# Rows of maxima in the second attention: one transfer inside SBUF in place of two through DRAM, and their transposition two pairs of score products later

## The reference, cut to what matters

```python
qw = split_heads(q @ Wq + bq); kw = split_heads(k @ Wk + bk); vw = split_heads(v @ Wv + bv)
scores = jnp.einsum('bhqd,bhkd->bhqk', qw, kw) * inv_sqrt_d
weights = jax.nn.softmax(scores, axis=-1)
ctx = jnp.einsum('bhqk,bhkd->bhqd', weights, vw)
ctx = ctx.transpose(0, 2, 1, 3).reshape(B, S, D_MODEL)
return ctx @ Wo + bo
```

## Time and profile before

| | |
|---|---|
| median of 3 runs | 1082.23 us (1081.29 to 1084.33) |
| the profiled execution, its own time | 1093.17 us |
| its span | 1091.1 us |
| mean granted clock of TensorE in it | 0.911 of full |
| TensorE, VectorE, ScalarE busy | 87%, 66%, 42% of the span |

### The profile page before, as it was taken

One profiled execution on the slowest core, in us unless ns is written; L12 is line 12 of the kernel. 1 busy time (PEld: TensorE's weight loads), 2 busy tenths in 40 slices (PEclk: granted clock), 3 DMA queues, 4 the chain that ended last, 5 costly groups with the idle time before them and its releaser, 6 DMA issues.

```text
span 1091.1 us, 19956 instructions
## 1 busy us (share of the span) xinstructions
PE 951.9 (87%) x6592; PEld 586.3 (54%) x6592; DVE 725.4 (66%) x1959; ACT 459.0 (42%) x1022; POOL 222.4 (20%) x198
## 2 busy tenths in 40 slices
PE   5989998998987999999998678889899787877785
PEld 3656666574754887888854433234343242345564
DVE  5473868578798666666644676687848776464676
ACT  4354543234225443444423203576646456622222
POOL 0313320101112443443210010100100011113453
PEclk9989999898988999999999956999959797788998
DMA  8541020026183111111126861722611036243231
GB/s 298 182 164 69 1 78 0 20 59 174 59 288 108 50 46 55 46 51 50 44 96 159 150 141 23 120 37 62 108 28 40 21 84 170 78 155 89 81 102 33
DMA packets 70239, 98.63 MB, mean 90 GB/s; under 512 B 8796, under 2 KB 57183, under 8 KB 67712
## 3 DMA queue, kind: packets, MB, share of 16 engines
q1 hardware_dynamic: 60000, 61.67, 20.7%
q0 software_dynamic: 10144, 35.69, 12.0%
HBM read 71.04 MB, written 27.15 MB: 90 GB/s over the span
## 4 chain that ended last, share of the span: by engine, by line
PE 61%; DVE 22%; ACT 6%; DMA 4%; issue 3%; another core or an unknown queue 2%; SPq 0%; ACTq 0%; POOLq 0%; DVEq 0%
PE pb L1050 11%; PE pb L1070 7%; PE pb L1162 4%; PE pb L883 4%; PE pb L1071 4%; PE pb L1186 3%; PE pb L1140 3%; PE pb L836 3%; PE pb L872 3%; PE pb L892 3%; PE pb L813 3%; PE pb L849 3%; DVE MX L2051 2%; PE pb L807 2%; ACT EX L1477 2%
## 5 line engine op out<-in xcount | busy, mean ns | idle before, releaser
L2051 DVE TENSOR_REDUCE MX<-pb 128x1 f32<-128x512 f32 x256 | 160.5, 683 | 47.0 <-PE pb L1140 45.7
L1415 ACT ACTIVATE m<-pb,b1m 128x128 f32<-128x128 f32 x404 | 114.9, 369 | 173.4 <-PE pb L1050 143.6
L1477 ACT ACTIVATE EX<-pb 128x512 f32<-128x512 f32 x256 | 137.0, 600 | 105.4 <-PE pb L1186 104.1
L1050 PE MATMUL pb<-xt,w1h 128*128 128x128 f16 x1616 | 157.3, 221 | 5.9 <-issue 3.8
L1070 PE MATMUL pb<-w,mh 128*128 x404 | 150.0, 381 | 10.1 <-DVE ml L1948 9.5
L1050 PEld LDWEIGHTS pb<-xt,w1h 128*128 x1616 | 120.4, 99 | 43.7 <-issue 8.3
L1050 PE MATMUL pb<-xt,w1l 128*128 128x128 f16 x808 | 113.2, 221 | 1.4 <-issue 1.3
L1071 PE MATMUL pb<-w,ml 128*128 x404 | 110.4, 273 | 0.4 <-issue 0.4
L807 PE MATMUL pb<-identh 128*128 128x512 f16 x373 | 96.7, 413 | 15.3 <-DVE identh L1585 7.4
L1186 PE MATMUL pb<-QS,KS 49*128 49x512 f32 x256 | 80.3, 505 | 13.3 <-ACT EX L1477 8.8
L1140 PE MATMUL pb<-KS,QS 48*128 48x512 f32 x256 | 71.4, 531 | 12.2 <-DVE MX L2051 8.0
(11 more groups left out here) (320 smaller groups left out, 1536.3 us busy)
## 6 DMA issues: line engine op xcount, KB each, us to landing
SR<-in_w1m SPq DMA_DIRECT2D x20, 512.0 KB, 5.4
SR<-in_w2m SPq DMA_DIRECT2D x12, 512.0 KB, 5.1
KS<-kd SPq DMA_DIRECT2D x48, 128.0 KB, 6.7
QS<-qd POOLq DMA_DIRECT2D x18, 256.0 KB, 9.1
kd<-KHL POOLq DMA_DIRECT2D x8, 512.0 KB, 5.7
vd<-VAB POOLq DMA_DIRECT2D x4, 1024.0 KB, 4.3
rows<-HL POOLq DMA_DIRECT2D x8, 512.0 KB, 3.9
GB<-outs SPq DMA_DIRECT2D x8, 512.0 KB, 7.5
```

What stands on the lines that cost most here:

```text
L1050: ins = pe.matmul(k.ap[:, h4 * TOK:(h4 + 1) * TOK], wt[:, bass.ds(regs[j], 128)], M.xt[j % 2][:, xc, :], start=i == 0, stop=i == 5)
L1415: ins = act.activation(M.m32[x % 2][:, h4, :], k.ap[:, h4 * TOK:(h4 + 1) * TOK], M.func, bias=M.b1[:, bass.ds(reg + 4 * g + h4, 1)], scale ...
L1477: act.activation(EX[m % len(EX)][:, i, :], k.ap, ACT.Exp, scale=0.25).then_inc(k.out, 1)
L2051: v.tensor_reduce(mx[:, t, 2 * s + j:2 * s + j + 1], k.ap, AX.X, ALU.max).then_inc(k.out, 1)
```

## The change

The DRAM tensor `md` goes. SP copies every second row of `MTR` straight into row 48 or 112 of `QS`, in two transfers per half as before, and waits only until `MTR` is written. On all engines the transposition, the negation and the copy of a half move from right behind its 16 pairs to behind the second pair of the next half (which may be the next batch's); only the very last half keeps them at its end. The wait of TensorE for the last pair's reductions moves with them. VectorE, which waited for the previous write to `md` before it overwrote `MTR`, now waits for the previous copies into `QS`. A half has 32 yields now, and the rate is 1.0.

```diff
-        md = nc.dram_tensor("md", (NB, NH, S), F32, kind="Internal").ap()
@@ order
-                beside(p["attend"](b, tails), (ms, 66 / 64), (side, 1.0), (early, 1.1), drain=False)
+                beside(p["attend"](b, tails), (ms, 1.0), (side, 1.0), (early, 1.1), drain=False)
@@ SP
+            def rows_out(b, half):
+                w.wait_ge(*M.take().ev)
+                for j in range(2):
+                    load(f"qm{b % 2}{half}", QS[b % 3][64 * j + 48:64 * j + 49, 4 * half:4 * half + 4, :].bitcast(F32),
+                         MTR[j:8:2, :].bitcast(F32))
+
             def maxima(b):
                 for half in range(2):
-                    for t in range(4):
-                        for _ in range(4):
-                            M.skip(2)
-                            yield
-                            yield
-                    w.wait_ge(*M.take().ev)
-                    load("md", md[b][8 * half:8 * half + 8], MTR[0:8, :].bitcast(F32))
-                    w.wait_ge(sem("d_md"), n["md"])
-                    for j in range(2):
-                        load(f"qm{b % 2}{half}", QS[b % 3][64 * j + 48:64 * j + 49, 4 * half:4 * half + 4, :].bitcast(F32),
-                             md[b].rearrange("(s j) n -> j s n", j=2)[j:j + 1, 4 * half:4 * half + 4])
+                    for i in range(16):
+                        if i == 2 and b + half:
+                            rows_out(b - 1 + half, 1 - half)
+                        M.skip(2)
+                        yield
+                        yield
+                if b == NB - 1:
+                    rows_out(b, 1)
                     yield
@@ TensorE
+            last_pair = []
+
+            def rows_out(b, half):
+                for k in last_pair:
+                    w.wait_ge(*k.ev)
+                transpose4(psum_m, [MXB[b % 2][:, t, 8 * half:8 * half + 8] for t in range(4)])
+
             def maxima(b):
...
+                            if t == 0 and s == 4 * half + 2 and b + half:
+                                rows_out(b - 1 + half, 1 - half)
                             ks = [psum_m.take() for _ in range(2)]
...
-                    for k in ks:
-                        w.wait_ge(*k.ev)
-                    transpose4(psum_m, [MXB[b % 2][:, t, 8 * half:8 * half + 8] for t in range(4)])
+                    last_pair[:] = ks
+                if b == NB - 1:
+                    rows_out(b, 1)
                     yield
@@ VectorE
+            def rows_out(b, half):
+                k = psum_m.take()
+                w.wait_ge(*k.mm)
+                if half:
+                    w.wait_ge(sem(f"d_qm{b % 2}0"), 32 * (b // 2 + 1))
+                elif b:
+                    w.wait_ge(sem(f"d_qm{1 - b % 2}1"), 32 * ((b - 1) // 2 + 1))
+                v.tensor_scalar(MTR[0:8, :], k.ap[0:8, 0:S], -1.0, None, ALU.mult, ALU.bypass).then_inc(k.out, 1)
...
-                    k = psum_m.take()
-                    w.wait_ge(*k.mm)
-                    w.wait_ge(sem("d_md"), 16 * (2 * b + half))
-                    v.tensor_scalar(MTR[0:8, :], k.ap[0:8, 0:S], -1.0, None, ALU.mult, ALU.bypass).then_inc(k.out, 1)
```

More of the change, by code:

```diff
@@ L1461, in maxima @@
                 for half in range(2):
-                    for _ in range(16):
+                    for i in range(16):
+                        if i == 2 and b + half:
+                            psum_m.skip(1)
                         psum_m.skip(2)
@@ L2321, in pool_program @@
                        combine_begin=nop, combine=lambda b: pause(6), first_loaded=nop, clear=nop, norms=nop, qprep=qprep,
-                       load_v=lambda b: pause(1), maxima=lambda b: pause(66), attend_loads=nop, attend=attend, wg_norm=nop, gate=gate,
+                       load_v=lambda b: pause(1), maxima=lambda b: pause(64 + (b == NB - 1)), attend_loads=nop, attend=attend, wg_norm=nop, gate=gate,
                        attend_done=nop, finish=nop))
```

## The result

The changed kernel takes 1072.11 us (median of four runs, 1067.61 to 1074.35), against 1083.28 us (1081.29 to 1085.53) of the kernel before beside it: ratio 0.9885, 95% interval 0.9839 to 0.9931. It is 11.2 us faster; forecast were 7.6 (1074.6 us, from 1068 to 1081.5). So a part of what the two profiles differ by is not typical, and the stages have to show which.

A forecast was written before the change was run, and what follows sets the result against it. TensorE was taken to set the pace, so its idle time counts as kernel time. 1.15 + 0 + 1.20 + 2.63 + 1.18 + 1.46 = 7.6 us off the median 1082.23 gave 1074.6 us, range 1068 to 1081.5.

The forecast's parts named there:

- if the clock stays low after step 16: Sign that the prediction is wrong: TensorE's clock staying low behind step 16 of batch 0.
- VectorE takes over: Rival, chance 0.2: VectorE limits the halves, saved stops return as waits for reductions; gain 4 us, 1078, up to 1081.
- (0, 0): Transposition ahead of the attention: VectorE's 1.15 us of idleness go; gain 1.15 us.
- (0, 1): Batch 0: the transposition's stop goes, but the stall before step 16 grows from 2.43 to 3.6 us; gain 0.
- (1, 0): Batch 1, no group of reads near: the transposition no longer stops TensorE; gain 1.20 us.
- (1, 1), (2, 0): At (1, 1) no stop, 0; at (2, 0) the second trip goes, gain 2.63 us, TensorE still waits 0.6 us.
- (3, 0): Batch 3: the transposition no longer stops TensorE; gain 1.18 us.
- Rest: Bank taken out of turn and the rate of 1.0: priced at 0, bounds -1 and +1 us.
- (3, 1): Last half's end: SP drops the trip to DRAM ahead of the weight chunks ScalarE waits for; gain 1.46 us.
- the clock falls: Rival, chance 0.15: the longer stall at batch 0's step 16 sets TensorE to 1.2 GHz; slower or no gain.
- the one-fold clock case: TensorE stays at 1.2 GHz behind batch 0's step 16 only, costing 9.3 us: 1083.9 us.
- the copies pass the reads: Rival, chance 0.15: copies of (0, 1) get through GpSimd's large packets, step 16's stall goes, up to 3.6 us more: 1071.

The follow-up runs named there:

- copy_only: The kernel before with MTR copied inside SBUF into QS, the transposition left right behind its 16 pairs; 1076.87 us, ratio 0.9884 to the kernel before.
- before_again: The kernel before, unchanged, run once more for a second profile; 1067.28 us, ratio 0.9968 to the kernel before.
- fillers: The changed kernel with 14 filler products ahead of step 16 of batch 0; 1051.52 us, ratio 0.9821 to the kernel before.
- move_only: The changed kernel with the rows still written to md and read back, the transposition two pairs later; 1079.11 us, ratio 0.9921 to the kernel before.
- before_fillers: The kernel before with 8 filler products ahead of batch 2's first step; 1066.33 us, ratio 0.9954 to the kernel before.
- one_pair: The changed kernel with the transposition one pair later in place of two; 1064.85 us, ratio 0.9803 to the kernel before.

## Why the prediction was right, and where it was off

The time fell into the range, and most of the sum's places behaved as forecast. But the prediction had named as a sign of being wrong "if the clock stays low after step 16", and it did. The points below take the sum first and the clock behind it.

- **What bounds the kernel** held. In the attention TensorE's idle time was worth its length, and pairs did not begin to wait for reductions: the rival "VectorE takes over" fell, with waits of 0.7 us at most and VectorE at 68% of the span. (Its price is slightly off: half of (2, 0) is 1.3 us, not 1.5, and no sum gives its "up to 1081".)
- **(0, 0), 1.15 us forecast.** From GpSimd's reads to batch 0 it took 22.08 us before and 22.09 in `copy_only`, 19.87 in the changed kernel and 19.29 to 19.81 in the other four of the table with the move: 2.2. Of these 0.8 are clock, since the 14 fillers at the end took 5.94 us before and 5.12 after. From the reads to the first filler it was 16.21 (in `before_again` 16.22) and 14.82: 1.4. Right, and a little small.
- **(0, 1), 0 forecast.** Right in mechanism and nearly in size: the stop went, the stall grew to 3.94 (forecast 3.6), and the half took 34.76 in place of 35.44, the clock being 0.93 in place of 0.90. At 0.94 `before_again` took 33.77, so at an equal clock the half loses up to a microsecond. The copies were issued 0.77 us behind the reads, not 1.0 to 2.4; that would have been enough either way. But they didn't land near the group's end, as the signs had it: their packets came out in the middle of it.
- **(1, 0), 1.20 forecast.** The stop went, but the clock hides the gain in the changed kernel's own stage. In `fillers`, at full clock, the stage took 24.09 us, against 25.45 in `copy_only`, which keeps the stop: 1.4.
- **(1, 1), (2, 0): 2.63 forecast.** Batch 1 with the stall at its end took 58.23 in place of 60.92: 2.69. The remaining stall was 1.10, not 0.6.
- **(3, 0), 1.18 forecast.** The stop went; the stage took 2.33 us less. Of the 1.15 beyond the stop 0.97 are the router's wait for its weights, 4.54 to 3.57. It is the term "Rest", priced at 0 with a bound of +1: the rate of 1.0 leaves one reduction fewer ahead of the router. `copy_only` against `move_only` shows that it comes with the move.
- **(3, 1), 1.46 forecast.** SP issues `SR` 1.72 us after the copies, and ScalarE's wait is gone, with TensorE's wait for `EX` of 1.1 us behind it. But the 1.46 don't show in the time. From the transposition to step 16 of batch 3 it took 20.79 us after, and 20.79 as well in `move_only`, which keeps the trip and in which ScalarE waits 1.11 us for `SR`: in the changed order the trip costs TensorE nothing. In the old order it was 22.82 in the first profile, but 21.22 in `before_again` and 21.38 in `before_fillers`, against 21.40 in `copy_only`, all at a clock of 0.92 to 0.93. TensorE's wait for `EX` is gone in `copy_only`, and one of 1.42 us for ScalarE's `XT` stands in that stretch, which the first profile has and the other two don't. The 0.4 to 0.6 us that are gone after came with the move and a clock of 1.00. This is the term of the sum that the runs don't bear out: ScalarE's wait was real, but its end did not set TensorE's pace.
- **The clock.** This is the step that failed in part: "I take it that the runs mostly don't have them, and count no gain." `before_again` shows that the kernel before has such stretches behind both stalls, with changing lengths. The rival "the clock falls", at 0.15, came true in its mechanism as well: behind step 16 the changed kernel ran at 1.2 GHz for about 15 us, in each of its profiles, and that costs 5.45 us. The remaining stall at batch 2 set nothing off. Before and after both pay, at different places: 10.7 and 16.0 us in the two profiles of the kernel before. That these two unpriced terms cancelled in part, and didn't turn the sign, is luck as far as the forecast goes.
- **The size.** Put together, the places measured 1.4 + 0 + 1.4 + 2.7 + 2.3 + 0.4 = 8.2 us. The result is 11.2, and 3 are left for the clock on both sides and for the measurement, whose interval spans 10 us. The runs don't divide that further. The stated range leaves out more than it says: the one-fold clock case, 1083.9, lies outside it too, and the first rival's far end, 1070.4, within.
- **The rival "the copies pass the reads"** came true in the change by half: at (0, 1) the copies' packets did get out among the large ones, but too late, and the stall stayed (11.4 us). In `one_pair`, at a lead of 0.89 us, they got out ahead of them and the stall went. Its 3.6 us more were under-priced, since the clock behind the stall (5.45 us) goes with it.

The place of the transposition gives and takes at once. Later, it costs no stop; but two pairs later its copies fall behind GpSimd's reads, which `copy_only` had them 0.64 us ahead of. That is why the copy alone did as well as both parts together.

## What to carry to other kernels

Where a few kilobytes share the DMA engines with a large group from another queue, compare the issue times first. Here the last packet of the same copies came 2.0 us after the issue at a lead of 0.89 us (and with no reads beside it), 4.0 at a lead of 0.64, and 9.4 when issued 0.77 us behind. A stall of TensorE is to be priced twice, with its length and with the clock behind it, and a single profile doesn't tell the second price of a typical run. When a change has two parts, run each alone: here one of them undid part of the other, and half the distance of the move kept the gains of both.

## What was not expected of the hardware

- Behind a stall the clock stayed at 1.2 GHz for some 10, 15, 24 and 34 us, with TensorE busy all the time (4.00 of 4.00 us in the windows from 704 and 728 above). In the same program at the same place it was 3.4 us in one profile and 34 in the other. What sets the length, these runs don't show.
- Small packets of SP's queue came out between the large ones of GpSimd's at (0, 1), and only behind them at (2, 0), in the kernel before (at (0, 1) 16 packets of SP's beside 105 of GpSimd's from 694 to 702; the earlier trace rows for (2, 0)) as in the changed one.
- The granted clock differed from execution to execution in an unchanged stretch, 0.71 and 0.89 in the windows shown, worth 4.45 us.
- The kernel before had medians of 1070.6 to 1089.8 us in the groups, 1.8% apart. The stretch behind the second attention, which nothing here changes, took 138 to 141 us in the profiles of the first result and the first group and 122 to 125 in those of the other two groups. Only ratios within a group tell anything at this size.
